# Expert tiles from a token table: gathers of single rows in place of indirect writes of all rows

## The chip, the cores and the metric

The kernel runs on one core of a Trainium2 chip. Time is device microseconds (us) of one execution. The engines are TensorE (PE; its weight loads are PEld), VectorE (DVE), ScalarE (ACT), GpSimd (POOL) and SyncE (SP), which here only issues DMAs. ACT and POOL issue DMAs too.

## The reference

Four layers follow each other on x of shape (8, 256, 128), fp32: attention with rope, an ffn layer, a second attention ("cov", whose scores are a covariance of q and k), and the same ffn layer again. Each has 16 heads of 8. The ffn layer is what the change is about:

```python
h = x + attention(layer_norm(x, ln1_w, ln1_b), w_qkv, b_qkv, w_o, b_o)
return h + moe_ff(layer_norm(h, ln2_w, ln2_b), w_gate, w1, b1, w2, b2)
# moe_ff, on t of 2048 tokens x 128:
probs = softmax(t @ w_gate)              # 8 experts
tw, ti = top_k(probs, 2); tw = tw / sum(tw)
for e in range(8):
    we = sum(where(ti == e, tw, 0.0))
    out = out + we[:, None] * (gelu(t @ w1[e] + b1[e]) @ w2[e] + b2[e])
```

## The kernel before

Work on a layer goes by blocks of 256 tokens (eight blocks, two pieces of 128 each). A software pipeline of 21 steps covers an attention layer and the ffn layer behind it; in one step TensorE, ACT, DVE and POOL each do a different stage of up to six blocks, named u, t, a, m, n, p from oldest to newest. For a block, `do_max` finds row maxima of raw scores (DVE), `do_exp` takes exp (ACT), `do_outT`, `divide` and `do_wo` finish attention, `close` normalises the result into U (POOL), `do_gate` and `choose` pick two experts per token.

After the pipeline comes the mixture, once per ffn layer (ph 0 and 1). Tokens are sorted by expert in two halves of four blocks. A half has 1024 tokens with two places each, so 2048 rows, padded per expert to 23 tiles of 128 rows (NTL). The sort of a half is `copy_totals`, `count_tiles`, `place_rows` and `name_experts` on DVE, with `do_rank` on TensorE; its result is SLOT (the place of every token's two rows) and EID (the expert of each tile). The first half's sort stands in the step where block 6 is at stage a (`ranking`), the step before the last; the second half's stands in the tile loop (`drain`, tiles 4 and 5).

`scatter` (L1581) then writes every row of U twice to its place in DRAM, sixteen indirect DMAs of 128 rows per half, on POOL's queue. Rows that nobody writes hold zeros: SP fills both tables once at the start. `load_x` (L395, SP) loads four tiles at a time into XT. It waits for all sixteen writes of the half, and SP executes in order, so loads of expert weights W (`load_w`, L406) behind it wait too.

On TensorE a group of four tiles is transposed (`turn_x`, L702), copied by ACT (`copy_x`, L943), and each tile goes through `hidden` (L714), gelu on ACT (L952) and `outputs` (L727), three tiles ahead; DVE evacuates (L1332), ACT stores. `gather` (L1601, POOL) fetches finished rows back, `combine` (DVE) adds them to X. In the first mixture the next layer's first blocks are started between tiles (`fill`). Three PSUM banks of a ring serve products that DVE reads, four those that ACT reads; a product waits until its bank was read. The order on each engine is written out by hand.

Of the kernel before, what the change touches and what calls it, by code (L numbers as in the profile page):

```python
# [11 lines left out]
P = 128  # L12
# [35 lines left out]
NGRP = len(GROUP)  # L48
GROUP_OF = {first: q for q, (first, _) in enumerate(GROUP)}
# [67 lines left out]
def build(nc, d, out):  # L117
    ctx = ExitStack()
    with ctx:
# [46 lines left out]
        R1 = sb("R1", [P, 3, TT, H, HD])  # L166
        R2 = sb("R2", [P, 3, TT, H, HD])
# [27 lines left out]
        sortc = sb("sortc", [P, 3 * P + E + E * E + NTL])  # L195
# [3 lines left out]
        tile_no = sortc[:, 3 * P + E + E * E:3 * P + E + E * E + NTL]  # L199
        totals = sb("totals", [P, P])  # L200
# [10 lines left out]
        sorted_u = [nc.dram_tensor(f"sorted_u{k}", (NTL * P, D), F32).ap() for k in range(2)]  # L211
# [27 lines left out]
        x_in = [sem(f"x_in{k}") for k in range(NXG)]  # L239
# [3 lines left out]
        scattered = [sem(f"scattered{k}") for k in range(2)]  # L243
        zero_set = sem("zero_set")
        zeroed = sem("zeroed")
# [48 lines left out]
        sorted_ = BlockEvent(sem("sorted"), 13, 2)  # L294
# [32 lines left out]
        EARLY, PACE_AT = 4, 5  # L327
        PACE = {n: (NB - 2, 10 + 2 * n) if n < 4 else (NB - 1, 2 * n - 6) for n in range(1, 12)}
# [4 lines left out]

        def ranking(a):

            return a and LAYERS[a[0]] == "ffn" and a[1] == NB - 2

# [13 lines left out]
        def own_steps(ph):  # L351


            return range(FILL if ph else 0, STEPS - DRAIN)

# [4 lines left out]
        def _(sp):  # L360
# [15 lines left out]
            sp.wait_ge(zero_set, 1)  # L376
            for half in range(2):
                sp.dma_start(sorted_u[half].rearrange("(i p) d -> p i d", p=P),
                             Yg[:, 0:1, :].broadcast_to([P, NTL, D])).then_inc(zeroed, 16)
# [8 lines left out]
            def load_x(ph, q):  # L388

                half, i = divmod(GROUP[q][0], NTL)  # L390
                n, k = GROUP[q][1], (ph * NGRP + q) % NXG
                if i == 0:
                    sp.wait_ge(scattered[half], 16 * GROUPS * (ph + 1))
                need(sp, x_turned, ph, q - NXG)
                sp.dma_start(XT[:, k, 0:n, :],  # L395
                             sorted_u[half][i * P:(i + n) * P, :].rearrange("(j p) d -> p j d", p=P)).then_inc(x_in[k], 16)

            def load_w(ph, at):
# [3 lines left out]
                if i == 0:  # L402
                    need(sp, sorted_, ph, half)
# [4 lines left out]
            for ph in range(2):  # L408
                for s in range(STEPS):
                    u, t, a, m, n, p = sequences(ph, s)  # L410
                    if a:
                        set_shift(*a, 1)
                    if m:
                        set_shift(*m, 0)
                for at in range(NW):
                    load_w(ph, at)
                for q in range(2 * NXG):
                    load_x(ph, q)
                for at in range(NAT):
                    if at + NW < NAT:  # L420
                        load_w(ph, at + NW)
                    if group_at(at - 1) is not None and group_at(at - 1) % (NGRP // 2) < NGRP // 2 - NXG:
                        load_x(ph, group_at(at - 1) + NXG)
                    if at == NTL - XG - 1:
                        for q in range(NGRP // 2, NGRP // 2 + 2 * NXG):
                            load_x(ph, q)
# [8 lines left out]
        def _(pe):  # L435
# [161 lines left out]
            def step(u, t, a, m, n, p):  # L597
# [39 lines left out]
                if ranking(a):  # L637
                    do_rank(a[0] // 2, 0, 1)
# [19 lines left out]
                if t:  # L658
                    do_onT(*t)

# [16 lines left out]
                if p and turned_ahead(p):  # L677
                    do_zT(*p)

# [16 lines left out]

            def turn_x(ph, q):
                x = ph * NGRP + q
# [1045 lines left out]
```

## Time and profile before

| | us |
|---|---|
| median of 3 runs (829.78 to 832.45) | 830.07 |
| profiled execution | 825.84 |
| its span | 824.0 |
| TensorE busy | 724.6 |
| DVE / ACT / POOL busy | 540.3 / 535.1 / 483.1 |

The span is what the engines' records cover; the execution's own time is a little longer. A line such as L727 is a line of the kernel; a matmul of fp32 counts as two instructions. Matmuls overlap, so a group of eight with 1.06 us ends some 0.9 us after it began for the next one.

### The profile page before, as it was taken

What the parts mean: (1) busy time and instruction counts of PE and PEld (TensorE: products, weight loads), DVE (VectorE), ACT (ScalarE), POOL (GpSimd) and SP (SyncE); (2) the same over time, 40 slices, a digit from 0 to 9 for tenths busy, and PEclk for the clock granted to TensorE, in tenths of its full rate; (3) what the DMA queues carried; (4) which work ended last, traced back from release to release, by engine and by line L of the source; (5) the groups of instructions that cost most, each with busy time, mean ns of one, the idle gap of its engine ahead of it and who ended that gap; (6) DMA issues with size and microseconds to landing.
All of it is one profiled execution on the core that took longest, in us unless ns stands there. A gap on an engine that the chain in (4) does not pass through costs nothing.

```text
span 824.0 us, 21303 instructions
## 1 busy us (share of the span) xinstructions
PE 724.6 (88%) x7166; PEld 547.9 (66%) x7166; DVE 540.3 (66%) x1370; ACT 535.1 (65%) x1264; POOL 483.1 (59%) x906
## 2 busy tenths in 40 slices
PE   1999999999999969989887998999999996999960
PEld 1765665666676559989865565666666654899950
DVE  5689999888989623112576888888888973311222
ACT  0277777787887737646546667777878873865630
POOL 6657778877754561505755665865686357060536
PEclk9789999999999979999989999999999997999985
DMA  9400000000000245667110000000000015486832
GB/s 274 144 2 3 2 4 3 3 3 3 3 4 3 69 138 155 205 182 216 54 35 14 15 18 8 3 3 3 3 4 3 3 35 162 126 231 180 256 91 70
DMA packets 57657, 56.29 MB, mean 68 GB/s; under 512 B 6856, under 2 KB 42448, under 8 KB 57552
## 3 DMA queue, kind: packets, MB, share of 16 engines
q1 hardware_dynamic: 39200, 39.13, 16.7%
q0 software_dynamic: 4096, 8.40, 3.4%
q10 hardware_dynamic: 14256, 7.41, 3.1%
q8 instruction: 61, 1.00, 0.5%
q14 instruction: 44, 0.36, 0.2%
HBM read 40.10 MB, written 14.29 MB: 66 GB/s over the span
## 4 chain that ended last, share of the span: by engine, by line
PE 52%; DVE 19%; POOL 14%; issue 8%; DMA 3%; ACT 2%; SPq 0%; ACTq 0%; POOLq 0%; DVEq 0%
DVE M L1110 11%; PE bankR L727 9%; PE bankE L714 9%; PE bankO L477 8%; PE bankE L450 7%; PE bankE L496 6%; PE bankR L463 4%; POOL Yg L1601 2%; POOL sorted_u L1581 2%; PE bankE L702 1%; DVE X L1343 1%; PE bankR L517 1%; POOL R L1475 1%; PE bankE L487 1%; POOL Zhl L1458 1%
## 5 line engine op out<-in xcount | busy, mean ns | idle before, releaser
L1110 DVE TENSOR_REDUCE M<-bankR 128x2 f32<-128x512 f32 x512 | 326.9, 684 | 58.8 <-PE bankR L463 56.0
L839 ACT ACTIVATE Pr<-bankE 128x512 f32<-128x512 f32 x512 | 275.9, 594 | 101.8 <-PE bankE L450 101.2
L463 PE MATMUL bankR<-KQ 32*128 32x256 f32 x1024 | 168.7, 336 | 13.5 <-DVE M L1110 5.5
L477 PE MATMUL bankO<-Pr,Vx 128*32 128x256 f32 x2048 | 139.2, 389 | 2.3 <-ACT OT L833 1.3
L450 PE MATMUL bankE<-KQ 32*128 32x256 f32 x1024 | 139.7, 331 | 1.3 <-ACT Pr L839 1.1
L450 PEld LDWEIGHTS bankE<-KQ 32*128 32x128 f32 x1024 | 85.4, 186 | 78.0 <-issue 46.2
L1332 DVE COPY Yb<-bankR 128x128 f32<-128x128 f32 x92 | 26.8, 291 | 156.3 <-PE bankR L727 150.2
L463 PEld LDWEIGHTS bankR<-KQ 32*128 32x128 f32 x1024 | 104.0, 189 | 31.1 <-DVE M L1110 25.8
L952 ACT ACTIVATE G<-bankE,W 128x128 f32<-128x128 f32 x368 | 101.0, 378 | 20.3 <-PE bankE L714 19.6
L1581 POOL DMA_INDIRECT sorted_u<-U,SLOT x64 | 62.3, 974 | 82.4 <-DVE past L1312 43.1
L1601 POOL DMA_INDIRECT Yg<-sorted_y,SLOT x64 | 62.1, 970 | 81.5 <-DVE Yb L1332 57.8
L714 PE MATMUL bankE<-XTT,W 128*128 128x128 f32 x736 | 101.5, 285 | 8.0 <-ACT G L952 3.3
L727 PE MATMUL bankR<-w,G 128*128 x736 | 98.7, 279 | 2.4 <-DVE Yb L1332 1.8
L714 PEld LDWEIGHTS bankE<-XTT,W 128*128 128x128 f32 x736 | 92.9, 200 | 11.1 <-issue 5.1
L727 PEld LDWEIGHTS bankR<-w,G 128*128 128x128 f32 x736 | 90.3, 194 | 3.7 <-issue 3.4
L833 ACT ACTIVATE KQ<-bankE 128x512 fp32r<-128x512 f32 x128 | 70.5, 607 | 34.1 <-PE bankE L496 32.2
L477 PEld LDWEIGHTS bankO<-Pr,Vx 128*32 128x32 f32 x2048 | 53.9, 110 | 42.4 <-issue 2.9
L943 ACT ACTIVATE XTT<-bankE,lncols 128x512 f32<-128x512 f32 (+1 forms) x24 | 18.3, 762 | 52.3 <-PE bankE L702 52.3
L1417 POOL TENSOR_SCALAR lnsmall<-meanvar 128x2 f32<-128x2 f32 x48 | 11.1, 230 | 68.1 <-DVE meanvar L1040 65.5
L496 PE MATMUL bankE<-ident_r,Kst 128*128 128x256 f32 (+1 forms) x256 | 39.9, 302 | 4.5 <-POOL Kst L1495 4.5
L496 PEld LDWEIGHTS bankE<-ident_r,Kst 128*128 128x128 f32 x256 | 35.2, 206 | 9.0 <-POOL Kst L1495 5.0
L496 PE MATMUL bankE<-ident_r,Qst 128*128 128x256 f32 (+1 forms) x256 | 38.4, 294 | 2.6 <-POOL Qst L1515 2.5
(169 smaller groups left out, 1089.3 us busy)
## 6 DMA issues: line engine op xcount, KB each, us to landing
W<-in_w1b SPq DMA_DIRECT2D x92, 258.0 KB, 3.2
sorted_y<-Yb ACTq DMA_DIRECT2D x92, 64.0 KB
XT<-sorted_u SPq DMA_DIRECT2D x20, 256.0 KB, 2.9
sorted_u<-Yg SPq DMA_DIRECT2D x2, 1472.0 KB, 9.9
KQ<-MT SPq DMA_DIRECT2D x128, 4.0 KB
X<-in_x SPq DMA_DIRECT2D x8, 128.0 KB, 7.2
sorted_u<-U,SLOT POOLq DMA_INDIRECT x64
Yg<-sorted_y,SLOT POOLq DMA_INDIRECT x64, 2.6
```

Source lines behind the costliest of these rows:

```text
L450: k = mm(act_bank("S", layer, b, h)[:, z * T:z * T + T], KT[rows, kb, g, z * P:z * P + P], QT[rows, kb, g, :], start=True, stop=True)
L463: k = mm(dve_bank("raw", layer, b, h)[:, z * T:z * T + T], QT[rows, kb, g, z * P:z * P + P], KT[rows, kb, g, :], start=True, stop=True)
L477: k = mm(bankO[SL * j:SL * j + SL, cols], Vx[:, b % VB, kc, HG * g + j, :], Pr[:, g % 2, j, kc, :], start=(g % 2 == 0 and kc == 0), stop=( ...
L496: return mm(bank[:, i * P:i * P + n], src, ident_r[:, 0:n], start=True, stop=True)
L714: k = mm(act_bank("hid", ph, at)[:, c * P:c * P + P], W1[:, n % NW, c * P:c * P + P], XTT[:, (ph * NGRP + q) % 2, j, :], start=True, stop= ...
L727: k = mm(dve_bank("out", ph, at)[:, 0:D], G[:, (ph * NAT + at) % NGB, c, :], w2[:, bass.ds(e * FC + c, 1), :].rearrange("p o d -> p (o d)" ...
L833: return nc.scalar.activation(dst, src, ACT.Copy)
L839: nc.scalar.activation(Pr[:, (h // HG) % 2, h % HG], act_bank("S", layer, b, h).rearrange("p (k q) -> p k q", k=TT), ACT.Exp, scale=EXP_SC ...
L952: nc.scalar.activation(G[:, n % NGB, c, :], act_bank("hid", ph, at)[:, c * P:c * P + P], ACT.Gelu_apprx_tanh, bias=W1[:, n % NW, FF + c:FF ...
L1110: v.tensor_reduce(M[:, b % 2, :, h], dve_bank("raw", layer, b, h).rearrange("p (t k) -> p t k", t=TT), AX.X, ALU.max, negate=True).then_in ...
L1581: g.indirect_dma_start(sorted_u[half][:, :], bass.IndirectOffsetOnAxis(ap=SLOT[:, half, n:n + 1], axis=0), U[:, b, t, :], None).then_inc(s ...
L1601: g.indirect_dma_start(Yg[:, n % NYG], None, sorted_y[half][:, :], bass.IndirectOffsetOnAxis(ap=SLOT[:, half, at:at + 1], axis=0)).then_in ...
```

## The change

U is no longer written row by row. After `close`, SP stores a block of U plainly to `u_rows` (`keep_rows`), and a table TOK of 128 x 23 says for every place of a half's tiles which token stands there. Each tile is then fetched by one indirect gather on POOL (`fetch_rows`), 23 per half in place of 16 writes and 6 loads. Places that no row owns get token 0. The zero fill goes. Six group buffers are used per half: XT for two, and memory of KQ, free by then, for four.

TOK is made on chip: DVE splits the place of a row into tile and row in tile (`split_places`, five operations), compares the row number with 0 to 127 for all sixteen groups (`mark_rows`, two operations on 1024 columns), and TensorE multiplies the two one-hot matrices, sixteen products of 24 columns (`find_owners`); DVE converts (`copy_owners`).

```diff
+            def find_owners(ph, half):
+
+                ring_r.take(pe, ("owners", ph, half))
+                bank = dve_bank("owners", ph, half)
+                for c in range(2):
+                    need(pe, sorted_, ph, half, 19 + c)
+                    for n in range(GROUPS // 2):
+                        g = c * GROUPS // 2 + n
+                        k = mm(bank[:, 0:NTC], in_row(c)[:, n * P:n * P + P],
+                               in_tile[:, g * NTC:g * NTC + NTC], start=g == 0, stop=g == GROUPS - 1)
+                    k.then_inc(owned.sem, 1)
+                ring_r.give(("owners", ph, half), sorted_, ph, half, 21)
...
+            def mark_rows(ph, half):
+
+                need(dve, zT, 2 * ph + 1, NB - 1)
+                need(dve, sorted_, ph, half, 18)
+                for c in range(2):
+                    own = slice(c * GROUPS // 2, (c + 1) * GROUPS // 2)
+                    tt(in_row(c).rearrange("p (g r) -> p g r", g=GROUPS // 2),
+                       row_no.unsqueeze(1).broadcast_to([P, GROUPS // 2, P]),
+                       row_of[:, own].unsqueeze(2).broadcast_to([P, GROUPS // 2, P]),
+                       ALU.is_equal).then_inc(sorted_.sem, 1)
...
+            def fetch_rows(ph, half, q):
...
+                    if half:
+                        need(pool, x_turned, ph, q)
+                    elif ph:
+                        need(pool, x_turned, ph - 1, NGRP // 2 + q)
+                    if not half and q == 0 and j == 2:
+                        need(pool, exped, layer, NB - 1)
+                    if not half and q == 1 and j:
+                        need(pool, (outT, onT, wo)[j - 1], layer, NB - 1)
...
+                    if half:
+                        need(pool, evacuated, ph, 9 + 4 * at // 5)
+                    g.indirect_dma_start(x_tile(q, j), None, u_rows[half][:, :],
+                                         bass.IndirectOffsetOnAxis(ap=TOK[:, half, at:at + 1], axis=0)).then_inc(
+                        x_in[q], 16)
```

The first half's sort moves on DVE from the step before the last into the last step (`last_step`), behind its two maxima, and the table's operations follow; the second half's table is made at tiles 6 to 8 of the loop. The three rank products of `do_rank` move to the end of the step before the last.

DVE, from the end of the step before the last to the last step's `choose`; names are tiles, M the maxima, place and past the sort, On the divide. Before:

```order
L1131 TENSOR_TENSOR Hs<-bankR,Hs 128x256
L1037 BN_STATS stats<-Hs 128x6 x2
L1040 BN_AGGR meanvar<-stats 128x2 x2
L1110 TENSOR_REDUCE M<-bankR 128x2 x2
L1120 RECIPROCAL rden<-bankR 128x32
L1124 TENSOR_TENSOR On<-bankR,rden 128x4x32 x2
L1137 COPY LG<-bankR 128x16
L1229 MAX top<-LG 128x8 x4
```

Now, from `place_rows`' last operation on (count and place stand between the maxima and these):

```order
L1343 CAST SLOT<-place 128x16
L1385 TENSOR_TENSOR past<-sortc,last 128x184
L1388 TENSOR_REDUCE npast<-past 128x23
L1390 TENSOR_SCALAR EID<-npast 128x23
L1350 TENSOR_SCALAR tile_of<-place 128x16
L1353 TENSOR_SCALAR tile_of<-tile_of 128x16
L1355 SCALAR_TENSOR_TENSOR row_of<-tile_of,place 128x16
L1357 TENSOR_TENSOR R<-sortc,tile_of 128x384
L1360 TENSOR_TENSOR R<-R,sortc 128x384
L1155 RECIPROCAL rden<-bankR 128x32
L1159 TENSOR_TENSOR On<-bankR,rden 128x4x32 x2
L1368 TENSOR_TENSOR Zhl<-sortc,row_of 128x1024
```

Seventeen operations now stand between the maxima and the divide, and two comparisons, the second into R, between the divide and the copy of the gate's logits (LG).

TensorE, the last step from the gate's product on. Before:

```order
L584 MATMUL bankR<-w_gate,UT 128x8 x2
L557 MATMUL bankE<-ident,On 128x128 x2
L450 MATMUL bankE<-KQ 128x256 x4
L477 MATMUL bankO<-Pr,Vx 32x256 x8
L450 MATMUL bankE<-KQ 128x256 x4
```

Now:

```order
L600 MATMUL bankR<-w_gate,UT 128x8 x2
L573 MATMUL bankE<-ident,On 128x128 x2
L723 MATMUL bankR<-R,Zhl 128x24 x8
L723 MATMUL bankR<-R 128x24 x8
L466 MATMUL bankE<-KQ 128x256 x4
```

The sixteen table products stand ahead of the step's last two pairs of scores.

TensorE at the start of a half: `turn_x` of the second group moves behind the first three tiles, and on ACT its copy behind the third tile's gelu.

```diff
                     turn_x(ph, half * NGRP // 2)
-                    turn_x(ph, half * NGRP // 2 + 1)
                     for at in range(half * NTL, half * NTL + LEAD):
                         hidden(ph, at)
+                    turn_x(ph, half * NGRP // 2 + 1)
...
+                    copy_x(ph, half * NGRP // 2)
                     for x in range(2):
-                        copy_x(ph, half * NGRP // 2 + x)
                         hidden(ph, half * NTL + x)
...
                         if at % NTL + 2 < NTL:
                             hidden(ph, at + 2)
+                        if at % NTL == 0:
+                            copy_x(ph, half * NGRP // 2 + 1)
```

On POOL the gathers of the first eight tiles stand behind the normalisation of block 5, four behind block 6's, the rest behind block 7's; those of the second half are spread over tiles 9 to 26 of the loop.

## Rows read from the trace of the kernel before

**Rows 1.** The page: busy us by engine; the indirect writes: busy us, mean ns.

```profile
PE 724.6 (88%) x7166; PEld 547.9 (66%) x7166; DVE 540.3 (66%) x1370; ACT 535.1 (65%) x1264; POOL 483.1 (59%) x906
...
L1581 POOL DMA_INDIRECT sorted_u<-U,SLOT x64 | 62.3, 974 | 82.4 <-DVE past L1312 43.1
```

**Rows 2.** Waits of PE by releaser: us in total, times, longest.

```profile
PE bankE L702 <- DMA XT<-sorted_u: 12.2, 2, 6.2
...
PE bankE L714 <- DMA W<-in_w1b: 2.6, 2, 1.9
```

**Rows 3.** PE timeline, first mixture's start: start us, us, work, idle before.

```profile
285.85 0.50 PE L450 MATMUL bankE<-KQ 32*128 32x256 f32 x4
...
289.31 0.64 PE L477 MATMUL bankO<-Pr,Vx 128*32 128x256 f32 x8 [0.53 <-ACT Pr L839]
...
294.68 0.71 PE L565 MATMUL bankR<-w_o_ffn,OnT 128*128 128x128 f32 x4
...
309.21 1.06 PE L727 MATMUL bankR<-w,G 128*128 x8
```

**Rows 4.** The same, second mixture's start.

```profile
688.80 0.71 PE L565 MATMUL bankR<-w_o_ffn,OnT 128*128 128x128 f32 x4
...
703.81 1.10 PE L727 MATMUL bankR<-w,G 128*128 x8
```

**Rows 5.** VectorE timeline: last two attention steps, then the second half's sort.

```profile
278.58 1.26 DVE L1110 TENSOR_REDUCE M<-bankR 128x2 f32<-128x512 f32 x2
282.88 0.36 DVE L1120 RECIPROCAL rden<-bankR 128x32 f32<-128x32 f32 x1 [3.05 <-PE bankR L547]
...
322.81 0.17 DVE L1277 TENSOR_SCALAR ntiles<-bankR 128x8 f32<-128x8 f32 x1 [0.38 <-PE bankR L694]
...
325.74 0.18 DVE L1317 TENSOR_SCALAR EID<-npast 128x23 uint32<-128x23 f32 x1
```

**Rows 6.** Windows: length, busy us of PE to POOL, granted clock, DMA share.

```profile
261.26:277.10 15.84, 14.11 (x158) 8.83 (x157) 14.69 (x45) 11.08 (x24) 6.13 (x10) 1.00 0.04 12
301.60:306.00 4.40, 4.37 (x19) 3.94 (x20) 0.00 (x0) 2.35 (x4) 2.17 (x6) 0.50 0.40 120
354.90:361.20 6.30, 4.01 (x35) 3.59 (x33) 0.29 (x1) 3.95 (x12) 0.00 (x0) 1.00 0.66 186
361.20:366.00 4.80, 4.80 (x26) 4.65 (x27) 0.29 (x1) 1.95 (x8) 0.00 (x0) 0.64 0.92 289
749.50:754.70 5.20, 4.03 (x34) 3.60 (x33) 0.29 (x1) 3.21 (x10) 0.00 (x0) 1.00 0.63 167
```

**Rows 7.** Gathers L1601 to landing; small products L584, ns min/median/max.

```profile
L584 PE MATMUL bankR<-w_gate,UT x64: 175/256/277, 210.2 to 709.8; 128*128 128x8 f32 x64
...
DMA to landing us min/median/max: 2.5/2.6/4.6
```

**Rows 8.** Rope products L1094 and VectorE on 512 columns, L1324: ns min/median/max.

```profile
L1094 DVE TENSOR_TENSOR R<-QKV,ropeB x24: 409/419/959, 16.8 to 137.3; 128x256 f32<-128x256 f32 x24
...
L1324 DVE TENSOR_TENSOR X<-bankR,X x8: 690/692/692, 293.3 to 746.9; 128x512 f32<-128x512 f32 x8
```

**Rows 9.** ACT timeline, first mixture: gelu's table, a copy of X, gelu of a tile.

```profile
303.56 1.28 ACT L952 ACT_TABLE_LOAD   x1
...
355.57 0.78 ACT L943 ACTIVATE XTT<-bankE,lncols 128x512 f32<-128x512 f32 x1 [4.09 <-PE bankE L702]
357.65 1.14 ACT L952 ACTIVATE G<-bankE,W 128x128 f32<-128x128 f32 x4 [1.31 <-PE bankE L714]
```

**Rows 10.** PE timeline around the change of halves, first mixture.

```profile
327.51 1.06 PE L727 MATMUL bankR<-w,G 128*128 x8
...
354.93 1.04 PE L702 MATMUL bankE<-ident,XT 128*128 128x128 f32 x8
...
361.20 1.16 PE L714 MATMUL bankE<-XTT,W 128*128 128x128 f32 x8 [1.86 <-DMA W<-in_w1b]
```

**Rows 11.** The same, second mixture.

```profile
754.73 1.16 PE L714 MATMUL bankE<-XTT,W 128*128 128x128 f32 x8 [0.77 <-DMA W<-in_w1b]
```

More of the change, by code:

```diff
@@ L165, in build @@
         QKV = sb("QKV", [P, 3, TT, D])
-        R1 = sb("R1", [P, 3, TT, H, HD])
-        R2 = sb("R2", [P, 3, TT, H, HD])
+        R_r, R = sb2("R", [P, 2, 3 * TT * H * HD])
+        R1, R2 = (R[:, k].rearrange("p (c t h x) -> p c t h x", c=3, t=TT, h=H) for k in range(2))
         hsq = sb("hsq", [P, 2 * TT * H])
@@ L210, in build @@
         EID = sb("EID", [P, 2, NTL], U32)
-        sorted_u = [nc.dram_tensor(f"sorted_u{k}", (NTL * P, D), F32).ap() for k in range(2)]
+        tile_of = sb("tile_of", [P, GROUPS])
+        row_of = sb("row_of", [P, GROUPS])
+        TOK = sb("TOK", [P, 2, NTL], U32)
+        u_rows = [nc.dram_tensor(f"u_rows{k}", (HB * T, D), F32).ap() for k in range(2)]
         sorted_y = [nc.dram_tensor(f"sorted_y{k}", (NTL * P, D), F32).ap() for k in range(2)]
@@ L238, in build @@
         w_cov = sem("w_cov")
-        x_in = [sem(f"x_in{k}") for k in range(NXG)]
+        x_in = [sem(f"x_in{k}") for k in range(XBUF)]
+        u_out = [sem(f"u_out{k}") for k in range(2)]
         w1_in = [sem(f"w1_in{k}") for k in range(NW)]
@@ L326, in build, with x_tile, last_step @@
         FILL, DRAIN = 3, 2
-        EARLY, PACE_AT = 4, 5
-        PACE = {n: (NB - 2, 10 + 2 * n) if n < 4 else (NB - 1, 2 * n - 6) for n in range(1, 12)}
         def block_of(u):
             return (u[0] // 2, u[1] // 2) if u and LAYERS[u[0]] == "ffn" and u[1] % 2 else None
+        def x_tile(q, j):
+            if q % (NGRP // 2) < NXG:
+                return XT[:, q % (NGRP // 2), j, :]
+            at = (q % (NGRP // 2) - NXG) * XG + j
+            return as32(KQ[:, at // 8, 0].rearrange("p g x -> p (g x)")[:, (at % 8) * D:(at % 8) * D + D])
         def ranking(a):
             return a and LAYERS[a[0]] == "ffn" and a[1] == NB - 2
+        def last_step(a):
+            return a and LAYERS[a[0]] == "ffn" and a[1] == NB - 1
         def group_at(at):
@@ L402, in load_w @@
                 if i == 0:
-                    need(sp, sorted_, ph, half)
+                    need(sp, sorted_, ph, half, 13)
                 e = sp.value_load(EID[0:1, half, i:i + 1], min_val=0, max_val=E - 1)
@@ L412, in _ @@
                         set_shift(*a, 1)
+                    if u and s < STEPS - DRAIN:
+                        keep_rows(*u)
                     if m:
@@ L416, in _ @@
                     load_w(ph, at)
[L417 to L426, printed above, removed]
+                for b in range(NB - DRAIN, NB):
+                    keep_rows(2 * ph + 1, b)
+                for at in range(NW, NAT):
+                    load_w(ph, at)
             dst = out.rearrange("b (t p) d -> p b t d", p=P)
@@ new lines, in fetch_rows @@
+                for j in range(GROUP[half * NGRP // 2 + q][1]):
+                    at = q * XG + j
+                    if at == 0:
+                        need(pool, sorted_, ph, half)
+                        pool.wait_ge(u_out[half], 16 * HB * (ph + 1))
+                    if half:
+                        need(pool, x_turned, ph, q)
[5 more added lines that the diff above has]
+                        need(pool, (outT, onT, wo)[j - 1], layer, NB - 1)
+                    if not half and q == NXG and j == 0:
+                        need(pool, scores, layer, NB - 1)
+                        need(pool, raw, layer, NB - 1)
+                    if half:
[3 more added lines that the diff above has]
+                        x_in[q], 16)
```

138 lines of the change are left out of this document (81 added, 57 removed).

## The prediction

> **What bounds the kernel now.** The page comes first: TensorE is busy for 724.6 of 824.0 us, every other engine for two thirds or less [rows 1]. So the time is TensorE's, and the second view is its list of waits. After the kernel's start the two largest that this change touches are 12.2 us for XT in two pieces and 2.6 us for W in two [rows 2]. The third view is TensorE's timeline at those places. In the first mixture the last attention product ends at 294.68 + 0.71 = 295.39, TensorE stands for the 6.2 us of the longer XT wait, and the first output product starts at 309.21, 13.8 us after that end [rows 3]. In the second it is 689.51 to 703.81, 14.3 us [rows 4]. Ahead of that, VectorE holds twelve sort instructions; the same twelve run without a gap from 322.81 to 325.92 in the second half, 3.1 us [rows 5]. The load of XT can only follow the last indirect write's landing. Last I read the granted clock: 0.50 for the 4.4 us behind the XT wait, which is 1.2 GHz of 2.4, and again 0.64 from 361.2 to 366, partly at that level [rows 6].
>
> **The change, part by part.** All times are set against the profiled execution, 825.84 us with a span of 824.0.
>
> *Writes and reload go.* POOL loses 64 writes of 0.97 us [rows 1] and gains 92 gathers of L1601's kind, taken at the same length, one every 1.25 us, and landing 2.6 us after their issue [rows 7]. The 35 us more (28 x 1.25) lie on an engine that is 59% busy and are taken at nothing. So are the new plain stores of U (SP issues them between the shift DMAs) and the zero fill that goes.
>
> *The two last attention steps.* The step before the last is VectorE's: 14.69 us busy of 15.84 [rows 6], and products there wait for banks that it frees. It loses the 3.1 us sort. Three rank products of 0.8 us move to that step's end, so I take 2.3 us: the last two max reductions, which now end at 278.58 + 1.26 = 279.84 [rows 5], end at 277.5. Then VectorE runs the sort (3.1), three small operations at 0.2 and two on 384 columns at 0.55 (512 take 0.69 [rows 8]), 1.7 together, and 0.5 for one collision with POOL, which normalises U there: a rope product takes 0.42 at the median and 0.96 at most [rows 8]. That is 282.8, just what the divide waits for now (282.88 [rows 5]), so the divide is not late. Behind it, at 283.6, come two comparisons on 1024 columns. No row has that size; 512 columns in 0.69 give 1.0 to 1.4, I take 1.25, hence 286.1. TensorE's second eight table products follow. Products of 8 columns last 0.26 [rows 7], a length in which neighbours overlap; between 0.05 and 0.2 apart, I take 0.1, so 287.0. Behind them stand scores that now start at 285.85 [rows 3]: 1.1 us late. About half returns in the 0.53 us that TensorE waits for exp at 289.31 [rows 3]. The last attention product then ends 0.5 us later than now; bounds -1.5 (all 2.3 us arrive) and +2.5 (none does).
>
> *The mixture's start, twice.* The table is copied at 287.1. POOL issues two gathers, waits for the last exp (about 289.8) with the third, and issues the fourth at 291.1; landed 293.7, before 295.9. The wait for XT goes. What is late next is ScalarE: four transposes and the copy, 1.45 us; gelu's table, 1.28; three tiles of gelu at 1.1; and only then the second copy, 0.75 [rows 9, 10]. The fourth hidden product starts 6.75 us after the attention ends, the first output product at 7.7, against 13.8 and 14.3. With the 0.5 from above 5.6 and 6.1 us are won.
>
> In those 6.75 us TensorE works for about 3.95. From 354.9 to 361.2 it worked 4.01 of 6.30 and the clock fell behind it; from 749.5 it worked 4.03 of 5.20 and the clock stayed [rows 6]. The new stretch is emptier than the one behind which it fell, so I expect a fall: the 4.8 us from 361.2 to 366 at 0.64 lost 4.8 x 0.36 = 1.7 us [rows 6], and that is my price for one. Left: 3.9 and 4.4, together 8.3 us.
>
> *The second half's table.* After the sort VectorE evacuates a tile (326.1), runs the 1.7 us of small operations, evacuates (328.1), compares for 2.5 us (330.6), and eight products end at 331.4. TensorE reaches this place at 327.51 + 0.9 = 328.4 [rows 10] and has the next hidden product queued behind. That is 3.0 us twice, 6.0; between 1.7 (sixteen products alone) and 4.
>
> *The change of halves.* Now the fourth hidden product starts 6.3 us after the transposes in the first mixture and 5.2 in the second, held by W [rows 10, 11]. SP no longer stands at a load of X ahead of W, so that wait goes. But the copy of the second group moves behind the third tile's gelu: gelu starts 2.7 us in (357.65 [rows 9]), three tiles and a copy end at 6.7. That is 0.4 and 1.5 us more, and 4.0 of 6.7 us busy means a fall of the clock in both; the first has one already, the second pays 1.7 more. Together 3.6 us.
>
> *Sum:* -8.3 + 6.0 + 3.6 = +1.3 us, 827.1 for the profiled execution. The runs' median stands 830.07/825.84 = 1.0051 above it, so **831.4 us**.
>
> One rule speaks against the change. The Trainium skill (SBUF — State Buffer, "SBUF: two separate sides") says that a VectorE operation with two SBUF inputs and a GpSimd operation that reads SBUF exclude each other for a whole instruction. The trace agrees in kind: 0.42 us becomes 0.96 in some rope products, in steps where POOL adds [rows 8]. By that rule several of the moved operations, not one, could each wait; as an estimate, four would add 1.5 us per mixture and make the sum +4.3.
>
> **Rivals.**
> *The clock stays up.* The stretch from 749.5 kept it [rows 6], and the new stretches have no row of their own. Then the three new falls (5.1 us) and the old one at 361 (1.7) are gone. But POOL becomes visible: its eighth gather waits for the last attention product (issue ends 296.9), block 6's normalisation takes about 3.4 (six short operations), four gathers 5.0, and block 7's U is there at 308.1, when TensorE wants it at 307.2; 0.9 twice. Sum -3.7: 826.4 us.
> *The table is cheap.* Comparisons at 1.0, products at 0.05, nothing lost in the last step, and the tile loop pays 1.7 rather than 3.0. For it speaks that TensorE's other small products overlap well; against it that the second table's wait is VectorE's queue. Sum 1.3 - 2.6 - 4.0 = -5.3: 824.7 us.
> *The table is late (slower).* The place is the last attention step. If the step before it is held by TensorE and ScalarE as much as by VectorE, taking out the sort wins nothing there, and the 7.8 us of sort, table and comparisons push the scores, the exp and the first gather 2.3 us later, in both mixtures. For it: that step's TensorE is also 14.11 us busy [rows 6]. Against it: part of this is products stretched by waiting. It decides once less than 1 us of the 3.1 returns. Sum +5.9: 836 us.
>
> **How the numbers follow.** Forecast 0.45, clock stays up 0.25, cheap table 0.10, late table 0.20. About 0.3% (2.5 us) is what a measurement can tell here. The forecast's own range is 828 to 835, mostly within 0.3%, else slower; the second case is mostly faster; the third faster; the fourth slower. That gives 0.33 faster, 0.36 the same, 0.31 slower, and 824 to 836.5 as the range.
>
> **What would show it.** Right: no wait of TensorE for XT; ScalarE's second copy of X behind three gelus, with TensorE waiting for it and clocks near 0.5 behind; about 3 us at the second table's products, released by VectorE; the last attention product about where it is now. Wrong: a step before the last as long as 15.8 us, gathers landing after the last attention product, or full clocks behind the waits for XTT.

## The result and the profile after

The changed kernel takes 837.84 us (median of 20 runs, 831.46 to 841.07), the kernel before 830.41 (20 runs). The ratio is 1.0077, with a 95% interval of 1.0054 to 1.010: slower by some 7.4 us, where +1.3 was forecast.

On the page TensorE's busy time grew by 20.7 us ([rows 1] has 724.6), and the gathers stand where the indirect writes stood:

```profile
PE 745.3 (89%) x7230; PEld 562.8 (67%) x7230; DVE 557.2 (67%) x1402; ACT 534.6 (64%) x1264; POOL 508.8 (61%) x933
...
L1665 POOL DMA_INDIRECT KQ<-u_rows,TOK x60 | 57.4, 956 | 35.6 <-DVE Yb L1405 21.6
```

TensorE's waits (releaser: us in total, times, longest). Those for XT's load and for W [rows 2] are gone; those for ScalarE's copy of X (XTT), POOL's U and VectorE's comparisons (Zhl) stand in their place:

```profile
PE bankE L745 <- ACT XTT L976: 5.8, 6, 1.5
...
PE bankE L591 <- POOL U L1506: 4.9, 2, 3.5
...
PE bankR L723 <- DVE Zhl L1368: 2.0, 4, 0.6
...
PE bankE L466 <- DMA KQ<-MT: 0.7, 1, 0.7
```

Where the time went is read best from windows that end at the same events in both kernels. For the first mixture they are, in this order: the step before the last attention step, the last step, the rest of the attention, the start (up to the first output product), the first half's tiles, the change of halves, the second half's tiles. Columns: length, busy us of PE, PEld, DVE, ACT and POOL, granted clock, DMA share, GB/s. The kernel before:

```profile
261.31:277.17 15.86, 14.13 (x160) 8.85 (x159) 14.71 (x44) 11.10 (x24) 6.13 (x10) 1.00 0.04 12
277.17:288.79 11.62, 10.88 (x118) 6.32 (x118) 5.49 (x33) 9.71 (x23) 8.92 (x14) 1.00 0.40 115
288.79:295.39 6.60, 6.08 (x50) 3.92 (x50) 3.36 (x11) 2.41 (x5) 5.08 (x6) 1.00 0.62 197
295.39:309.21 13.82, 7.59 (x41) 7.15 (x41) 1.17 (x6) 5.56 (x14) 7.46 (x16) 0.63 0.36 106
309.21:355.09 45.88, 45.20 (x399) 44.38 (x398) 12.97 (x60) 29.45 (x93) 15.46 (x16) 1.00 0.61 177
355.09:362.32 7.23, 4.94 (x41) 4.37 (x39) 0.29 (x1) 4.76 (x14) 0.00 (x0) 1.00 0.72 204
362.32:421.60 59.28, 53.99 (x424) 51.29 (x424) 25.40 (x66) 29.29 (x93) 35.23 (x60) 0.94 0.43 125
```

The changed kernel:

```profile
262.84:276.54 13.70, 12.63 (x150) 7.79 (x150) 12.00 (x31) 10.39 (x24) 2.98 (x7) 1.00 0.05 13
276.54:293.50 16.96, 15.57 (x140) 9.92 (x140) 13.08 (x54) 10.71 (x23) 5.11 (x9) 0.86 0.44 123
293.50:300.55 7.05, 7.04 (x52) 4.28 (x53) 3.27 (x10) 1.94 (x4) 4.71 (x5) 0.84 0.18 46
300.55:305.97 5.42, 4.55 (x42) 4.31 (x39) 1.17 (x6) 4.91 (x14) 4.54 (x9) 1.00 0.20 48
305.97:361.53 55.56, 50.73 (x415) 49.53 (x414) 16.70 (x68) 30.03 (x94) 30.74 (x37) 0.94 0.66 170
361.53:366.95 5.42, 4.55 (x41) 4.32 (x39) 0.29 (x1) 2.95 (x9) 3.07 (x4) 1.00 0.34 62
366.95:426.91 59.96, 53.30 (x424) 50.30 (x423) 25.64 (x66) 31.00 (x98) 40.32 (x65) 0.96 0.46 118
```

The reader is to see the start shrink from 13.82 to 5.42, and the two windows that pay for it: the last step, 11.62 to 16.96, and the first half's tiles, 45.88 to 55.56. Both hold a granted clock below 1.00, which they did not before. With the second mixture, read in the same way:

| us | before | after | both mixtures | forecast |
|---|---|---|---|---|
| attention, three windows | 34.08 / 34.08 | 37.71 / 39.81 | +9.4 | +1.0 |
| start | 13.82 / 14.30 | 5.42 / 7.92 | -14.8 | -12.7 |
| first half's tiles | 45.88 / 45.90 | 55.56 / 50.38 | +14.2 | +9.4 |
| change and second half | 66.51 / 45.90 | 65.38 / 46.24 | -0.8 | +3.6 |
| sum | | | +8.0 | +1.3 |

The forecast's 3.4 us for two clock falls behind the start stand with the first half's tiles. A profile is of one execution: that of the kernel before was 4.6 us faster than its median, that of the changed kernel 1.5 us slower, so it is partly luck that the table's 8.0 us lie near the medians' 7.4.

The profiled spans differ by 13.4 us; the 5.4 that this table lacks lie outside the mixtures. Of these, 2.0 us lie between the mixtures, where the clock was at half speed for 19.0 us, against 10.2 in the kernel before. Another 1.5 us lie ahead of the first mixture; there the changed kernel had less half speed (3.4 us for 17.1), and the kernel with the products alone, below, which is the kernel before up to that point, took 2.7 us more than it; so executions differ by as much. The last 1.8 us are the end, behind the last output product: 28.4 us in both profiles without the change, 30.2 to 32.5 in all twelve with it. There POOL's last gather and the instruction that closes POOL's work (duration in ns, start in us) read, before:

```profile
818.86 0.94 POOL L1601 DMA_INDIRECT Yg<-sorted_y,SLOT  x1 [0.30 <-issue]
...
L119 POOLq DRAIN  x1: 11935/11935/11935, 811.9 to 811.9; - x1
```

and in the changed kernel:

```profile
829.20 0.94 POOL L1685 DMA_INDIRECT Yg<-sorted_y,SLOT  x1 [0.30 <-issue]
...
L120 POOLq DRAIN  x1: 15092/15092/15092, 822.1 to 822.1; - x1
```

The DRAIN ends 4.0 us after the last gather in both profiles with 128 indirect DMAs, 7.0 us after it in all twelve with 156, and the engines' last instructions follow it. Of these 3.0 us, 1.2 are offset because the last gather ends sooner behind the last product (23.0 us for 24.2). Why the DRAIN takes longer was not tested.

TensorE's timeline in the changed kernel (start, us, work, idle before), one line of the last step's middle, then from the table products on; it answers to [rows 3]:

```profile
280.80 1.07 PE L493 MATMUL bankO<-Pr,Vx 128*32 128x256 f32 x16
...
286.92 1.03 PE L723 MATMUL bankR<-R,Zhl 128*128 128x24 f32 x8 [0.34 <-DVE Zhl L1368]
287.97 1.06 PE L723 MATMUL bankR<-R 128*128 128x24 f32 x8
288.96 0.80 PE L466 MATMUL bankE<-KQ 32*128 32x256 f32 x4
289.68 1.93 PE L493 MATMUL bankO<-Pr,Vx 128*32 128x256 f32 x16
...
305.97 1.06 PE L758 MATMUL bankR<-w,G 128*128 x8
...
312.99 0.69 PE L591 MATMUL bankE<-ident,U 128*128 128x128 f32 x2 [3.55 <-POOL U L1506]
313.47 1.92 PE L745 MATMUL bankE<-XTT,W 128*128 128x128 f32 x8
```

The scores at 285.85 now start at 288.96. All of the changed kernel lies 1.53 us later from 261 on (262.84 for 261.31 in the windows), so they are 1.6 us late by the change itself. What follows runs at half speed: 1.93 us for sixteen products of the same shape as sixteen that take 1.07 at 280.80, in the same step. The window is

```profile
289.00:295.60 6.60, 6.58 (x45) 3.17 (x48) 3.27 (x27) 2.28 (x6) 3.73 (x4) 0.50 0.65 191
```

POOL's timeline shows why block 7's U is late at 312.99: the eighth gather waits for the last attention product, block 6's normalisation follows, then four gathers, then block 7's.

```profile
300.83 0.94 POOL L1665 DMA_INDIRECT XT<-u_rows,TOK  x1 [0.78 <-PE bankR L581]
301.85 0.23 POOL L1495 TENSOR_SCALAR lnsmall<-meanvar 128x2 f32<-128x2 f32 x1
...
305.37 1.10 POOL L1665 DMA_INDIRECT KQ<-u_rows,TOK  x1 [0.16 <-issue]
...
312.05 0.88 POOL L1506 TENSOR_SCALAR U<-Hs,lnsmall 128x128 f32<-128x128 f32 x2
```

### The profile page after: what moved, and what is told of

Same layout as the page of the kernel before. It is cut to its first block, busy times and chain, and to the rows that moved or that the text cites. A ratio compares the mean times of both kernels' runs of the same rounds, so it can differ in the third digit from the quotient of the medians.

```text
span 837.4 us, 21545 instructions
## 1 busy us (share of the span) xinstructions
PE 745.3 (89%) x7230; PEld 562.8 (67%) x7230; DVE 557.2 (67%) x1402; ACT 534.6 (64%) x1264; POOL 508.8 (61%) x933
## 4 chain that ended last, share of the span: by engine, by line
PE 53%; DVE 21%; POOL 14%; issue 8%; ACT 2%; DMA 1%; ACTq 1%; POOLq 0%; DVEq 0%
DVE M L1145 10%; PE bankO L493 9%; PE bankR L758 8%; PE bankE L745 7%; PE bankE L466 7%; PE bankE L512 6%; PE bankR L479 4%; POOL Yg L1685 2%; POOL lnsmall L1497 1%; PE bankE L503 1%; PE bankR L581 1%; PE bankR L533 1%; DVE stats L1072 1%; PE bankR L723 1%; POOL Z L1506 1%
## 5 line engine op out<-in xcount | busy, mean ns | idle before, releaser
L493 PE MATMUL bankO<-Pr,Vx 128*32 128x256 f32 x2048 | 144.8, 402 | 0.7 <-ACT OT L866 0.7
L466 PE MATMUL bankE<-KQ 32*128 32x256 f32 x1024 | 143.1, 336 | 1.7 <-ACT Pr L872 0.9
L466 PEld LDWEIGHTS bankE<-KQ 32*128 32x128 f32 x1024 | 87.9, 190 | 80.5 <-issue 48.3
L1665 POOL DMA_INDIRECT KQ<-u_rows,TOK x60 | 57.4, 956 | 35.6 <-DVE Yb L1405 21.6
L1495 POOL TENSOR_SCALAR lnsmall<-meanvar 128x2 f32<-128x2 f32 x48 | 11.1, 230 | 89.3 <-DVE meanvar L1075 86.7
L1665 POOL DMA_INDIRECT XT<-u_rows,TOK x32 | 30.6, 956 | 51.6 <-DVE Yb L1405 22.1
```

What stands on the lines that cost most here:

```text
L466: k = mm(act_bank("S", layer, b, h)[:, z * T:z * T + T], KT[rows, kb, g, z * P:z * P + P], QT[rows, kb, g, :], start=True, stop=True)
L493: k = mm(bankO[SL * j:SL * j + SL, cols], Vx[:, b % VB, kc, HG * g + j, :], Pr[:, g % 2, j, kc, :], start=(g % 2 == 0 and kc == 0), stop=( ...
L1665: g.indirect_dma_start(x_tile(q, j), None, u_rows[half][:, :], bass.IndirectOffsetOnAxis(ap=TOK[:, half, at:at + 1], axis=0)).then_inc(x_i ...
```

## The experiments

Each is timed against its own runs of the kernel before; the changed kernel's ratio to compare with is 1.0077 (1.0054 to 1.010).

### Taking the first half's products away

```
-                if last_step(a):
-                    find_owners(a[0] // 2, 0)
...
-                v.tensor_copy(TOK[:, half], dve_bank("owners", ph, half)[:, 0:NTL]).then_inc(sorted_.sem, 1)
+                at = 4 * P + E + E * E + NTC + GROUPS - NTL
+                v.tensor_copy(TOK[:, half], sortc[:, at:at + NTL] if half == 0 else
+                              dve_bank("owners", ph, half)[:, 0:NTL]).then_inc(sorted_.sem, 1)
```

> The sixteen table products of the first half are left out in both mixtures; the table is copied from constants, so the rows gathered for the first half are others. Theory (the products stand on TensorE's path in the last attention step, and the half-speed stretch behind them is theirs): 2.4 us of products and wait and about 2 us of half speed go, twice, so 837.8 - 8.8 = 829 us, and the granted clock stays full from the last scores to the last attention product. Rival (the last step is late because the sort and the ranks stand there; the falls of the clock come anyway): only the 2.0 us of products go, twice, so 834 us, with a half-speed stretch as long as before.

831.36 us, ratio 0.9996 (0.9972 to 1.002). Windows of the last step and the rest of the attention in the first mixture:

```profile
276.63:289.55 12.92, 11.59 (x125) 7.08 (x124) 12.13 (x49) 9.86 (x22) 4.03 (x8) 1.00 0.31 79
289.55:296.44 6.89, 6.09 (x52) 4.11 (x53) 4.09 (x18) 2.69 (x6) 5.06 (x7) 1.00 0.74 193
```

The step is 4.0 us shorter than the changed kernel's and the clock is full; in the second mixture it is 12.29 against 17.31. Some 6.5 us go, between the two theories. Sort, ranks and comparisons are all still there, so it is the products, with what comes with them (the table, copied from constants, is also ready earlier). The half-speed stretches are not all gone: each mixture has 3.4 us in the start and 3.4 in the tiles.

### The products alone, in the kernel before

```
+            def spare(ph):
+
+                ring_r.take(pe, ("spare", ph, 0))
+                for g in range(GROUPS):
+                    k = mm(dve_bank("spare", ph, 0)[:, 0:24], ident_r[:, 0:P], ident_r[:, 0:24],
+                           start=g == 0, stop=g == GROUPS - 1)
...
```

> The kernel before with one thing added: sixteen products of 24 columns, of constants that are always there, at the place in the last attention step where the changed kernel has its table products; nothing reads them and nothing else is moved. Theory (these products, with the half-speed stretch that they bring, are what the last attention step lost): 2.0 us of their own and some 2 to 2.5 us of half speed, twice, so 830.4 + 8.5 = 839 us, with a half-speed stretch inside the last attention step. Rival (the step lost its time to the sort, the ranks and the comparisons that were moved into it): the products cost at most their own 2.0 us twice, 832 to 834.5 us, and the clock stays full until the attention ends.

832.54 us, ratio 1.0002 (0.9971 to 1.0033): no cost that can be told, and less than the products' own 3.9 us. The theory is wrong; the rival, which allowed up to twice 2.0 us, is not, though its full clock failed in the first mixture (below). TensorE's timeline has the products, and its waits the load of XT, two times 4.2 us where [rows 2] has 6.1:

```profile
686.66 1.93 PE L704 MATMUL bankR<-ident_r 128*128 128x24 f32 x16
```

```profile
PE bankE L714 <- DMA XT<-sorted_u: 8.4, 2, 4.4
```

In the kernel before the attention's end did not set the start; the load of XT did, and 2 us more of TensorE's work came out of that wait. The change took this cover away, and with it a late attention became time. The products also ran at full clock, with no fall in the 8 us behind them in either mixture. But in the first mixture the clock had just come back from a fall, ahead of the products, in the last attention step and the one before it (two windows: the last step; the fall):

```profile
281.44:297.54 16.10, 16.10 (x134) 9.98 (x134) 5.26 (x32) 9.85 (x22) 10.48 (x15) 0.72 0.45 140
277.00:290.60 13.60, 13.60 (x92) 7.46 (x92) 5.74 (x16) 6.87 (x14) 9.08 (x15) 0.50 0.13 38
```

Up to there this is the program of the kernel before, which ran the same steps at 1.00. So a fall in these steps comes without such products too, in some executions, and only the second mixture is a plain case of the products bringing none.

### The same products elsewhere, and in another form

Behind the last scores instead of ahead of the last but one:

```
-                if last_step(a):
-                    find_owners(a[0] // 2, 0)
...
                     do_qT(*n)
+                if last_step(a):
+                    find_owners(a[0] // 2, 0)
                 if t:
```

> The first half's table products two places later: behind the last scores instead of ahead of the last but one, with VectorE's copy of the table behind its weights. Theory (there they fill the time in which TensorE waits for exp, and no longer wait for the second comparison): about 1.2 us less twice, 835.5 us; with the half-speed stretch gone as well 831.5 us. Rival (the table, 2 us later, makes the first gathers late): a wait of TensorE for XT of 1 to 2 us takes it back, 837.8 us or more.

839.43 us, ratio 1.0082 (1.0052 to 1.0112). The last step is 15.10 and 14.29 us long, 1.9 and 3.0 less, and no wait for XT appears. But the clock falls behind the products here too, and the rest of the attention takes 7.90 and 8.07, the starts 7.56 and 7.52. The step's gain is real and the time does not show it.

Operands changed round, in place:

```
-                        k = mm(bank[:, 0:NTC], in_row(c)[:, n * P:n * P + P],
-                               in_tile[:, g * NTC:g * NTC + NTC], start=g == 0, stop=g == GROUPS - 1)
+                        k = mm(bank[0:NTC, 0:P], in_tile[:, g * NTC:g * NTC + NTC],
+                               in_row(c)[:, n * P:n * P + P], start=g == 0, stop=g == GROUPS - 1)
...
+                turn(bank[:, 0:NTC], past[0:NTC].rearrange("p i e -> p (i e)")[:, 0:P],
+                     ident[0:NTC, 0:NTC]).then_inc(owned.sem, 1)
```

> The table products with their operands changed round, in both halves: 24 columns loaded as weights and 128 columns moved, instead of 128 loaded and 24 moved; VectorE copies the result, one transpose turns it, and the second half's table is turned one tile later. Theory (their 0.13 us each is the load of 128 columns of weights; products of 32 loaded columns here run 16 in 1.07 us): 1.0 us less four times, 0.2 us for the transpose four times: 834.5 us, and 830.5 us if the half-speed stretch of the last attention step goes with it. Rival (0.13 us is the pace of such products either way): 838.5 us.

837.28 us, ratio 1.0057 (1.003 to 1.0084). The last steps, first and second mixture:

```profile
277.99:292.59 14.60, 12.81 (x142) 7.98 (x141) 12.64 (x51) 10.23 (x23) 3.00 (x8) 1.00 0.36 100
678.14:692.25 14.11, 12.83 (x141) 7.98 (x141) 12.15 (x51) 10.12 (x23) 3.13 (x8) 1.00 0.37 94
```

The rest of the attention is 6.61 in both, so the three attention windows together take 35.7 and 34.4 us, against 34.1 before and 37.7 and 39.8 after. Yet the time hardly moves: U is now waited for 2.6 us in each mixture, and each start has 6.8 us at half speed. One wait out of the way leaves the next. (The profiled execution took 841.98 us.)

### POOL's order

```
-                    if not half and q == 0 and j == 2:
-                        need(pool, exped, layer, NB - 1)
-                    if not half and q == 1 and j:
-                        need(pool, (outT, onT, wo)[j - 1], layer, NB - 1)
...
                         fetch_rows(ph, 0, 0)
-                        fetch_rows(ph, 0, 1)
                     if s == STEPS - DRAIN:
+                        fetch_rows(ph, 0, 1)
+                    if s == STEPS - 1:
                         fetch_rows(ph, 0, 2)
```

> POOL's order alone: four gathers, block 6's normalisation, four gathers, block 7's, and then the rest, and no gather waits for an attention product. Theory (block 7's U is late because eight gathers, one of them held for the last attention product, and four more stand ahead of it): TensorE's wait for U of 4.9 us in all and the half-speed stretch behind the longer one go, 5 to 8 us, so 830 to 833 us. Rival (the wait moves to the second group's gathers, which now issue behind block 6): a wait of TensorE for the second group of X of 2 to 3 us each time, 836 to 838 us.

839.81 us, ratio 1.0102 (1.0074 to 1.0129, 7 runs). The wait for U is gone; a wait for the third group of X (KQ) of 1.5 us takes its place in the first mixture, none in the second. The rival is nearer in time. The profiled execution took 833.64 us, 6 us under the median, so the waits of the others may be longer.

```
+                for t in range(TT):
+                    v.tensor_scalar(U[:, b, t, :], Hs[:, b, t, :], sm[:, 1, t:t + 1], sm[:, 3, t:t + 1],
+                                    ALU.mult, ALU.add).then_inc(ev.sem, 1)
...
-                    if s == STEPS - DRAIN:
-                        fetch_rows(ph, 0, 2)
                     if s == STEPS - 1:
+                        fetch_rows(ph, 0, 2)
```

> The last two blocks' U written by VectorE, which is idle there, instead of POOL; POOL still works out the moments, and both blocks' moments come ahead of the third group's gathers. Theory (TensorE's wait for block 7's U, 3.5 and 1.4 us, is POOL's queue): the wait and the half-speed stretch behind the longer one go, 833 to 835 us. Rival (POOL's queue only moves: the third group's gathers land later and TensorE waits for KQ): 836 to 838 us.

839.26 us, ratio 1.0078 (1.0041 to 1.0115). The first half's tiles come down to 49.83 and 50.31 us, with the wait for U gone and one of 1.0 us for KQ in each. The last attention steps were 17.78 us in both mixtures of this profile, and the time did not follow. Alone, neither edit helps.

### The change of halves, and the stores

```
                     turn_x(ph, half * NGRP // 2)
+                    if half:
+                        turn_x(ph, half * NGRP // 2 + 1)
...
+                        if half and x:
+                            copy_x(ph, half * NGRP // 2 + 1)
                         hidden(ph, half * NTL + x)
```

> The change of halves alone as in the kernel before: both transposes of X ahead of the third hidden product, and ScalarE's second copy ahead of the second tile's gelu. Theory of the prediction (the new order holds the fourth hidden product 0.4 and 1.5 us longer and lets the clock fall once more): 3.6 us faster, 834 us. Rival (the new order is as good or better there, since what held the products was the wait for weights, which went with the loads of X): 0 to 2 us slower, 838 to 840 us.

835.42 us, ratio 1.0057 (1.0028 to 1.0085): the interval overlaps the changed kernel's, so the time alone decides nothing. In the second mixture change and second half take 5.49 + 39.73 = 45.22 us, 1.0 less than the change's order, at full clock in both. So that order costs something, but not in the form foretold.

```
-                    if u and s < STEPS - DRAIN:
-                        keep_rows(*u)
                     if m:
                         set_shift(*m, 0)
+                    if s and s < STEPS - DRAIN:
+                        w = sequences(ph, s - 1)[0]
+                        if w:
+                            keep_rows(*w)
```

> SP's plain stores of U one step later, behind the shift DMAs. Theory (the store of 128 KB beside the shift DMA made TensorE wait 0.7 us for KQ in the last attention step): 0.7 us twice, 836.4 us, and no wait of TensorE for KQ. Rival (the shift lands late for another reason, or the scores behind it are held by exp anyway): 837.8 us.

836.27 us, ratio 1.008 (1.0052 to 1.0108). The median is the theory's, but the interval holds the rival's too, and the wait for the shift stays (1.1 us in the first mixture): the store beside it was not its cause, which stays open.

### All together, and each taken out again

The combined kernel has the edits above (operands changed round, stores later, the old order of the second half, and POOL's order as edited there), the second half's table a tile later, and the last two blocks' U on VectorE with only the power on POOL:

```
+                if LAYERS[layer] == "ffn" and b >= NB - 2:
+                    need(pool, u_ready, layer, b, 1)
+                    g.tensor_tensor(lnsmall4[:, 1], lnsmall4[:, 0], halves[:], ALU.pow).then_inc(u_ready.sem, 1)
...
-                if i == 8:
+                if i == 9:
                     find_owners(ph, 1)
```

> Together: the table products with operands changed round, the stores of U one step later, the last two blocks' U on VectorE with POOL giving the power alone, no gather held for an attention product, the second half's order of X as in the kernel before, and the second half's table one tile later. Theory (each cost that the traces showed is a wait or a product of its own, and they add up): per mixture the three attention stretches 34.4 us as with the changed operands alone against 34.1 before, the start 7 to 8.5 against 13.8 and 14.3, the first half's tiles 48 to 49 against 45.9, the change and the second half together 0.7 less: 3 to 5 us less each, so 822 to 826 us. Rival (the granted clock takes back what waits give: each emptied wait is followed by a half-speed stretch elsewhere): the same waits gone but 14 us or more at half speed around each start, 828 to 832 us.

824.53 us, ratio 0.9923 (0.9892 to 0.9954): faster than both kernels, 5.9 us under the kernel before. Its windows in the first mixture, last step and start to first half:

```profile
277.08:291.17 14.09, 12.82 (x142) 7.97 (x141) 12.13 (x51) 10.12 (x23) 3.06 (x8) 1.00 0.36 98
...
298.29:305.93 7.64, 6.77 (x41) 6.37 (x40) 2.71 (x11) 5.29 (x15) 6.13 (x7) 0.64 0.37 85
305.93:353.44 47.51, 46.80 (x416) 45.58 (x415) 16.98 (x69) 29.75 (x93) 25.78 (x28) 1.00 0.75 194
```

The seven windows sum to 154.8 us, against 160.3 before and 164.1 after. The rival is seen in small: the start still has 0.64 of the clock, and in the second mixture the last step has a fall too:

```profile
668.16:683.73 15.57, 14.29 (x141) 8.60 (x141) 12.13 (x51) 10.10 (x23) 3.07 (x8) 0.89 0.40 114
```

With the products in the change's form:

```
-                        k = mm(bank[0:NTC, 0:P], in_tile[:, g * NTC:g * NTC + NTC],
-                               in_row(c)[:, n * P:n * P + P], start=g == 0, stop=g == GROUPS - 1)
+                        k = mm(bank[:, 0:NTC], in_row(c)[:, n * P:n * P + P],
+                               in_tile[:, g * NTC:g * NTC + NTC], start=g == 0, stop=g == GROUPS - 1)
```

> The combined kernel with the table products as in the change (128 columns loaded, 24 moved; no transpose), all else the same. Theory (what those products cost is mostly the half-speed stretch behind them, which five of the seven kernels that had them in the last attention step ahead of the last scores showed): 0.4 us more of their own and 2.5 us of half speed in the last attention step, twice, 830 us. Rival (such stretches come as often with either form, and only lengths count): 0.4 us in the step and 0.7 in the tile loop, less the transposes' 0.4, twice: 826 us.

828.97 us, ratio 0.9968 (0.9938 to 0.9997): 4.4 us more by the medians, 3.7 by the ratios, whose intervals overlap a little (0.9938 and 0.9954); nine of the combined kernel's ten runs are under 825.7 us, ten of these twelve over 827. That is nearer the theory's 5.5 than the rival's 1.5, and the last step shows it:

```profile
276.11:293.38 17.27, 16.40 (x141) 10.84 (x140) 12.56 (x54) 10.61 (x23) 6.11 (x10) 0.81 0.45 122
```

17.27 us at 0.81, and 17.18 in the second mixture, against 14.09 at 1.00 and 15.57 at 0.89. Over the profiles, from the step before the last to the end of the first half's tiles, the kernels with this form ahead of the last scores ran 17.1 us at half speed (mean of twelve mixtures), those with operands changed round 11.1 (eight), the kernel before 10.2 (two). The kernel before with the products of constants had 23.9 and 10.2, the one without the first half's products 6.8 twice; single mixtures of one kernel differ by up to 13.7 us, so the two means are a tendency and no measure.

With POOL as in the change (it writes U, and gathers are held):

```
+                    if not half and q == 1 and j:
+                        need(pool, (outT, onT, wo)[j - 1], layer, NB - 1)
...
+                    moments(ev, layer, b, meanvar3[:, b % 2], lnsmall3, 0)
```

> The combined kernel with POOL as in the change: it writes the last two blocks' U between the gathers, and gathers wait for exp and for attention products. Theory (TensorE's wait for block 7's U is POOL's queue, and comes back): a wait of 1.3 to 3.5 us in each mixture and a half-speed stretch behind the longer ones, 828 to 832 us. Rival (with the attention shorter, POOL's U is not what TensorE waits for): 825 us.

832.47 us, ratio 1.0015 (0.9988 to 1.0042): 7.9 us more, the whole of the gain. Who writes U, the order of the gathers and what they wait for were put back at once, so the 7.9 us are theirs together. TensorE waits twice 2.5 us for U, and the first half's tiles take 51.22 and 55.20 us against 47.51 and 48.29, with the clock at 0.97 and 0.94:

```profile
PE bankE L593 <- POOL U L1536: 5.0, 2, 2.5
```

With the change's order at the change of halves:

```
-                    if half:
-                        turn_x(ph, half * NGRP // 2 + 1)
                     for at in range(half * NTL, half * NTL + LEAD):
                         hidden(ph, at)
-                    if not half:
-                        turn_x(ph, half * NGRP // 2 + 1)
+                    turn_x(ph, half * NGRP // 2 + 1)
```

> The combined kernel with the change's order at the change of halves (the second group of X behind the third hidden product on TensorE and behind three gelus on ScalarE). Theory (that order costs 1.0 us in the second half's tiles, as the profiles with the old order show): 2 us more, 826.5 us. Rival (the second half starts no later either way): 824.5 us.

825.35 us, ratio 0.9919 (0.9889 to 0.995). The profile has 65.67 and 46.41 us for change and second half, against 64.69 and 45.26: the 1.0 us is there, but no difference in time can be told from these runs.

## Why the prediction was wrong

**The step that failed** is "the last attention product then ends 0.5 us later than now; bounds -1.5 and +2.5". It ended 3.6 and 5.7 us later, so 8.4 us were missing there. The working on VectorE held. The step before the last gave back 2.2 us of the foretold 2.3 in the first mixture (1.2 in the second, where 3.4 us of it ran at half speed); less the 1.53 us by which all lies later, the divide came 0.4 us later than the forecast had it, and the comparisons took 1.21 and 1.22 us for 1.25. The one collision with POOL came too, in the first mixture:

```profile
281.00 0.92 DVE L1338 TENSOR_TENSOR rank<-rank,OH 128x128 f32<-128x128 f32 x1
...
285.56 1.21 DVE L1368 TENSOR_TENSOR Zhl<-sortc,row_of 128x1024 fp32r<-128x1024 f32 x1
286.69 1.22 DVE L1368 TENSOR_TENSOR R<-sortc,row_of 128x1024 fp32r<-128x1024 f32 x1
```

L1338 has two inputs in SBUF and took 0.92 us, where the second half's sort, with POOL elsewhere, has it at 0.29; in the second mixture's last step it took 0.38. The rule of the Trainium skill (SBUF — State Buffer, "SBUF: two separate sides") thus shows once there, not four times: +4.3 would have been nearer by the wrong term.

The table products run 0.13 us apart, not 0.1, so the last scores are 1.6 us late where 1.1 was forecast. The rest, 2.0 of the 3.6 us in the first mixture, is the clock: 0.50 from 289.0 to 295.6. The forecast put its three new falls behind waits and none in a step where TensorE is busy for 15.57 of 16.96 us. That the products are what costs there is shown by the kernel without them (0.9996) and by the combined kernel with and without their form (about 4 us). Why the clock falls in this step is not settled: the same form with constants, in the kernel before, brought no fall, that kernel had one ahead of its products, the combined kernel had one with the other form, and in one profile of the change's form (old order of the second half) the fall began 0.4 us ahead of the first product.

**The start** was foretold at 7.7 us and took 5.42 and 7.92, the second at a granted clock of 0.61. The wait for XT went, as said. The working had the fourth hidden product wait for the second copy of X. It belongs to the first group of four, so only the fifth can wait. A fall of the clock came in the second mixture as the attention ended, in the first later (at 313, behind the wait for U).

**The second half's table** took 2.7 us (from 330.4, when the output product's successor could start, to 333.13) against 3.0 forecast, in both mixtures; in the first the clock fell behind it.

**POOL at nothing** is the other wrong step. The first half's tiles cost 14.2 us more, not 9.4, and 4.9 of it is the wait for U. The prediction had that wait only in the rival where the clock stays up, at 0.9 us. It counted POOL's 35 us more (25.7 by the two pages) against an idle share of the span, when the question was what stands ahead of U in POOL's queue. Put back into the combined kernel, the change's part on POOL costs 7.9 us. The longer DRAIN at the kernel's end, 3.0 us in every profile with the change, the combined kernel's too, had no term at all.

**The change of halves** gave 0.8 us instead of costing 3.6. The wait for W went, the fourth hidden product came 4.7 us after the transposes in the first mixture instead of 6.7, and the clock was full (1.00 in that window). The wait for the second copy stands one product later, 1.5 us in the first mixture and 0.9 in the second; the old order saves about 1.0.

**The rivals.** "The table is late" came nearest in time, 836 us, by a mechanism that did not happen: the step before the last did give back its 2.2 us. "The clock stays up" came in part, at the changes of halves and in the first mixture's start, and it alone foresaw the wait for U, which became 3.5 and 1.4 us instead of 0.9 twice; but the clock fell in the attention and the tiles. "The table is cheap" did not come. Of the signs named for being wrong, full clocks behind waits for XTT were seen there.

## What to carry to other kernels

Removing a wait for a transfer also removes the cover that it gave to everything ahead of it: test each added instruction against the place with the wait gone, not against the kernel as it stands. An engine with a low busy share still has a queue in order; ask of each moved instruction what the engine does right behind it, and who waits for that. It can also hold the kernel's end, which no window inside the kernel shows. Single repairs here moved nothing measurable, since the next wait or a half-speed stretch took their place; only together were they worth 1.5%, and taking one out of the combined kernel priced it where adding it to the changed kernel could not.

## What the runs showed of the hardware

The table products cost by the columns that they load, not by those that they move. The weight loads of table products of both halves in the changed kernel's first mixture (us in total, mean ns of one):

```profile
L723 PEld LDWEIGHTS bankR<-R 128*128 128x128 f32 x16 | 1.9, 191 | 0.2
```

and in the combined kernel, with 24 columns loaded and 128 moved:

```profile
L728 PEld LDWEIGHTS bankR<-R 128*24 128x24 f32 x16 | 1.0, 102 | 0.6 <-DVE R L1393 0.6
```

Eight of them then follow each other in 0.66 us instead of 1.06 (TensorE's timeline of the combined kernel):

```profile
286.95 0.64 PE L728 MATMUL bankR<-Zhl,R 128*24 128x128 f32 x8 [0.42 <-DVE Zhl L1393]
288.00 0.66 PE L728 MATMUL bankR<-R 128*24 128x128 f32 x8 [0.40 <-DVE R L1393]
```

The Trainium skill (TensorE: Matmul & The Clock Gate, "LDWEIGHTS (loading the stationary operand)") lets the load's time go by its columns, P/1.2 ns: as an estimate from it, 107 and 20 ns. The trace agrees in the difference, 89 ns for 104 columns fewer against the estimate's 87, and has about 83 ns more in each.

No kernel came through a mixture at full clock: between the step before the last and the end of the first half's tiles each of the 28 profiled mixtures has at least 6.8 us at half speed, in the attention, in the start or in the tiles. Mending one stretch ended the falls in no kernel.
